# A decoder layer in fp32 on one core: SP's queue in another order, and half of k's moves on GpSimd

## The chip, the cores and the metric

The kernel runs on one core of one Trainium2 chip. The time is the device time of one execution in microseconds (us); several executions give a median. The core has five engines with instruction streams of their own: TensorE (PE, and PEld for its weight loads), VectorE (DVE), ScalarE (ACT), GpSimd (POOL) and SyncE (SP), which here only issues DMAs. They meet through semaphores.

## What is computed

One layer over x of 4 batches x 256 tokens x 256 channels, all in float32:

```
x = x + attention(layernorm(x))          # 32 heads of 64, 8 k/v heads, rotary embedding, causal
x = x + ssm(ctx, z = layernorm(x))       # selective scan over 256 steps, 256 channels, 16 states
x = x + ffn(layernorm(x))                # gate, up, down; int32 weights: (w - 128) * scale

attention: q, k, v = h Wq', h Wk', h Wv';  rope(q), rope(k);  softmax(q k' / 8, causal) v;  Wo
ssm:       u = silu(conv4(in_proj ctx));  dt, B, C = x_proj u;  delta = softplus(dt_proj dt + b)
           s_t = s_{t-1} exp(delta A) + delta u B_t;  y_t = s_t C_t;  (y + D u) silu(z)
ffn:       down(silu(gate h) * (up h))
```

## The kernel before, in words

Attention is cut into 32 **units** (UNITS, L36), one for each batch and k/v head; a unit holds the 4 q heads of its k/v head. Four units make a **k group** (KG): k is projected, rotated and moved for four units at once. The scan is cut into 32 pieces (16 states x 2 halves of the channels), laid under the units by the list SCANS (L56): none in units 0 to 3, then 1, 2, 1, 2, then one in each of units 8 to 28, and 2, 2, 1.

What TensorE does is written out in `unit` (L1171): transposes of the probabilities of unit u, the **scores** of unit u+1 (`scores`, L1031, its products at L1041), more transposes, pieces of the output projection (L1141), in the second unit of a group the projection (`fill`, L1028) of the next k group, in the third that of v, the product with v (L1123), and the projection of q for unit u+3. VectorE (`unit`, L850) rotates q for unit u+2 (`rope`, L698 and L699: two products, read from PSUM), scales the attention of unit u-1 (L809), takes the maxima of the scores of u+1 (L711), and runs the scan piece: the product with B (`drive`, L786), the scan (L793), in a group's second unit k's rotation (L701, L703), and the product with C (L799). ScalarE does the exponentials (L493), the copies out of PSUM (L499) and the scan's decays (L519). GpSimd (L443) adds the two halves of a rotation (`add_rope`, L418) and adds a scan piece to y (`add_y`, L424).

**Moves.** The rotation leaves q and k in `rc` with the two halves of a head in different places. Short DMAs of 32 KB bring them to `qt` and `kt`, where scores read them. For a unit's q these are 8 DMAs, 4 issued by SP and 4 by GpSimd (`move_heads`, L257, DMA at L266). For a k group these are 8 DMAs, all by SP (`move_k`, L295, DMA at L303); SP then waits for them and issues one more DMA of 256 KB that copies kt's lower 64 partitions to its upper ones (L306), the **doubling copy**, for which the group's first scores wait (`k_in`). The rotation buffer has two places, so VectorE's next rotation but one waits for the moves.

**SP's queue** (L273 to L364) is served in order, and a wait in it holds up all behind it. In the start: x, weights, k's moves and its copy, q's moves of units 0 and 1, more weights. Then B and C of the scan go out to DRAM and come back, broadcast to 128 partitions, as `bc` (two DMAs of 512 KB for each state, two buffers). Then q of unit 2, weights, q of unit 3, k group 1 with its copy, wo (2 MB), all the feed-forward weights and scales (L332 to L343), q of units 4 and 5, and the second bc. From unit 4 a loop (L349): q of unit u+2, in a group's second unit the next k group with wait and copy, and then the bc loads that unit u's own scans set free (L359, a wait for `hc_done`).

The integer weights are converted by VectorE at the end of unit 5 (gate, L821) and of unit 12 (up and down, L826, L830).

In the start ScalarE issues its loads, the last eight being Wq's for units 2 and 3 (L533), and then an activation that loads its table (L537, `act_warm`). GpSimd waits for that before it computes the layernorm's rstd (L393), and VectorE's normalisation (L681) waits for rstd.

## Time and profile before

| what | value |
|---|---|
| median of 3 runs | 524.07 us (522.26 to 529.78) |
| the profiled execution | 523.78 us, of which the profile's span is 522.0 us |
| busy: PE / PEld / DVE / ACT / POOL | 79% / 62% / 70% / 52% / 42% of the span |
| mean granted clock of TensorE | 0.912 |
| the chain that ended last, by engine | PE 33%, DVE 17%, issue 15%, SP's queue 12%, POOL 9%, DMA 7% |

Busy shares are means over the whole span. A unit starts with its scores: the time from one group of L1041 products to the next is the length of a unit. What ended an engine's idle time stands in brackets behind an instruction in the timeline, with the time it was idle. "SPq" marks a DMA's issue on SP's queue, which isn't counted as busy; a DMA lands later than it is issued.

### The profile page before, as it was taken

To read this page: it belongs to the slowest core of one execution; us is meant where nothing else is said; L and a number is where in the kernel's file an instruction comes from. 1 tells how busy PE (TensorE), PEld (TensorE's weight loads), DVE (VectorE), ACT (ScalarE), POOL (GpSimd) and SP (SyncE) were. 2 spreads that over 40 slices of the span, in tenths; PEclk is the share of its full clock that TensorE was granted. 3 is DMA by queue.
4 is the path that set the end of the run, shared out by engine and by line. 5 is a ranking of instruction groups with operands and counts; after the bars stand their busy time and mean duration, and the time that the engine had idled before them with its cause. 6 is when DMAs were issued, how large, how long until landed. Compare 5 with 4: busy or idle time off the path is not lost.

```text
span 522.0 us, 7681 instructions
## 1 busy us (share of the span) xinstructions
PE 414.5 (79%) x2604; PEld 325.4 (62%) x2636; DVE 366.6 (70%) x485; ACT 271.0 (52%) x779; POOL 221.3 (42%) x234
## 2 busy tenths in 40 slices
PE   3648987188768697987889799978998894659996
PEld 1433666166656476866777688757887773447774
DVE  2774357257999885897798679858767999755442
ACT  0514587046556465755666658645556665433321
POOL 1741232206464666446446635635464474310000
PEclk9787789687889799998999989989999997779999
DMA  9325324703151415201430521323042130000000
GB/s 223 74 56 96 113 51 131 230 10 98 37 170 55 156 31 153 96 11 46 133 102 24 144 91 48 76 87 102 21 133 74 57 102 0 2 0 21 20 22 20
DMA packets 51110, 40.63 MB, mean 78 GB/s; under 512 B 32280, under 2 KB 43744, under 8 KB 51072
## 3 DMA queue, kind: packets, MB, share of 16 engines
q1 hardware_dynamic: 40864, 34.48, 23.2%
q0 software_dynamic: 4096, 4.20, 3.4%
q10 hardware_dynamic: 6112, 1.47, 1.4%
q8 instruction: 21, 0.34, 0.3%
q14 instruction: 17, 0.14, 0.1%
HBM read 26.36 MB, written 1.18 MB: 53 GB/s over the span
## 4 chain that ended last, share of the span: by engine, by line
PE 33%; DVE 17%; issue 15%; SPq 12%; POOL 9%; DMA 7%; ACT 5%; ACTq 2%; DVEq 0%; POOLq 0%
PE ps_s L1041 6%; SPq L303 6%; PE ps_p L1028 6%; PE ps_p L1243 5%; DMA qt<-rc 4%; POOL rc L418 4%; DVE state L793 4%; PE ps_s L1228 3%; DVE nmax L711 3%; PE ps_p L1141 3%; PE ps_r L1095 3%; DVE state L786 3%; DMA kt<-rc 3%; SPq L266 2%; POOL y L424 2%
## 5 line engine op out<-in xcount | busy, mean ns | idle before, releaser
L493 ACT ACTIVATE prob<-ps_s,nmax 128x256 f32<-128x256 f32 (+1 forms) x256 | 104.8, 444 | 72.6 <-DVE nmax L711 72.6
L424 POOL TENSOR_TENSOR y<-y,state 128x1024 f32<-128x1024 f32 x32 | 80.3, 2510 | 112.2 <-DVE state L799 112.2
L418 POOL TENSOR_TENSOR rc<-rc,rs 128x512 f32<-128x512 f32 x40 | 57.7, 1442 | 104.0 <-DVE rs L699 70.4
L711 DVE TENSOR_REDUCE nmax<-ps_s 128x2 f32<-128x512 f32 (+1 forms) x96 | 60.3, 682 | 45.1 <-PE ps_s L1052 45.1
L499 ACT ACTIVATE pt<-ps_r 128x512 f32<-128x512 f32 x96 | 53.6, 593 | 58.1 <-PE ps_r L1095 54.5
L793 DVE TENSOR_TENSOR_SCAN state<-decay,state 128x1024 f32<-128x1024 f32 x32 | 81.5, 2546 | 2.3 <-ACT decay L519 1.2
L1041 PE MATMUL ps_s<-kt,qt 64*128 64x256 f32 (+1 forms) x512 | 55.5, 360 | 30.7 <-DMA qt<-rc 30.7
L1028 PE MATMUL ps_p<-xt_all,wq 128*128 128x256 f32 x256 | 71.2, 427 | 9.1 <-DVE rs L703 6.4
L1041 PEld LDWEIGHTS ps_s<-kt,qt 64*128 64x128 f32 x512 | 47.1, 201 | 38.2 <-DMA qt<-rc 32.5
L266 POOL DMA_DIRECT2D qt<-rc x128 | 63.8, 504 | 9.7 <-POOL rc L418 9.5
L1141 PE MATMUL ps_p<-wo,attn_t 128*128 128x256 f32 x256 | 61.7, 389 | 7.7 <-DVE x L816 4.1
L1095 PE MATMUL ps_r<-ident,prob 128*128 128x128 f32 x384 | 55.2, 282 | 14.8 <-ACT pt L499 12.6
L1028 PEld LDWEIGHTS ps_p<-xt_all,wq 128*128 128x128 f32 x256 | 51.5, 211 | 23.4 <-DVE rs L703 8.0
L1095 PEld LDWEIGHTS ps_r<-ident,prob 128*128 128x128 f32 x384 | 48.2, 147 | 20.3 <-ACT pt L499 13.2
L493 ACT ACTIVATION_READ_ACCUMULATOR prob<-ps_s,nmax 128x1 f32 x256 | 58.8, 230 | 0.0
L1141 PEld LDWEIGHTS ps_p<-wo,attn_t 128*128 128x128 f32 x256 | 47.8, 195 | 14.6 <-DVE x L816 4.8
L1123 PE MATMUL ps_o<-pt,vv 128*64 128x256 f32 x256 | 43.1, 415 | 12.5 <-ACT pt L499 12.4
L698 DVE TENSOR_TENSOR rc<-ps_p,cos_s 128x512 f32<-128x512 f32 x32 | 22.0, 689 | 34.0 <-PE ps_p L1028 23.0
L786 DVE TENSOR_TENSOR state<-du,bc 128x1024 f32<-128x1024 f32 x32 | 41.6, 1301 | 0.0
L799 DVE TENSOR_TENSOR state<-state,bc 128x1024 f32<-128x1024 f32 x32 | 38.8, 1214 | 0.2
L519 ACT ACTIVATE decay<-delta,a_neg 128x1020 f32<-128x1020 f32 x32 | 36.6, 1144 | 0.0
L506 ACT ACTIVATE x<-rinv 128x512 f32<-128x512 f32 x32 | 20.2, 631 | 22.7 <-DVE rinv L720 22.7
(110 smaller groups left out, 531.1 us busy)
## 6 DMA issues: line engine op xcount, KB each, us to landing
bc<-bc_scratch SPq DMA_DIRECT2D x32, 512.0 KB, 4.7
qt<-rc POOLq DMA_DIRECT2D x128, 32.0 KB, 1.7
qt<-rc SPq DMA_DIRECT2D x128, 32.0 KB, 2.0
kt<-rc SPq DMA_DIRECT2D x64, 32.0 KB, 1.8
kt<-kt SPq DMA_DIRECT2D x8, 256.0 KB, 3.0
wo<-wo_t SPq DMA_DIRECT2D x1, 2048.0 KB, 10.9
wq<-wqkv_t SPq DMA_DIRECT2D x24, 64.0 KB, 2.6
xs<-x SPq DMA_DIRECT2D x1, 1024.0 KB, 8.1
```

The source lines that it names most:

```text
L266: queue.dma_start(qt[to:to + HALF, u % 2, h // 2, :], rc[h * HALF:(h + 1) * HALF, r % 2, c, :]).then_inc(landed[u % 2], 16)
L418: nc.gpsimd.tensor_tensor(rc[:, r % 2, :, :], rc[:, r % 2, :, :], rs[:], ALU.add).then_inc(rope_add, 1)
L424: nc.gpsimd.tensor_tensor(y[:, v % 2, :], y[:, v % 2, :], state[:, v % 2, :], ALU.add).then_inc(state_free, 1)
L493: nc.scalar.activation(o, i, ACT.Exp, bias=nmax[:, r, c:c + 1], accum_out=rsum[:, r, GRP + head:GRP + head + 1]).then_inc(exp_done, 1)
L499: nc.scalar.activation(pt[:, fill, :], ps_r[:, fill % 2, :], ACT.Copy).then_inc(pt_copied, 1)
L711: nc.vector.tensor_reduce(nmax[:, u % 2, c:c + k], ps_s[:, part, :].rearrange("p (k s) -> p k s", k=k), AX.X, ALU.max, negate=True).then_i ...
L786: nc.vector.tensor_tensor(state[:, v % 2, :], du[:, v % 2, :], bc[:, n % 2, 0, :], ALU.mult).then_inc(drive_done, 1)
L793: nc.vector.tensor_tensor_scan(state[:, v % 2, :], decay[:, v % 2, :], state[:, v % 2, :], 0.0, ALU.mult, ALU.add).then_inc(decay_free, 1)
L1028: last = nc.tensor.matmul(o, lhs, rhs, start=(k == 0), stop=(k == KT - 1))
L1041: return nc.tensor.matmul(ps_s[:, bank, col:col + keys], qt[lo:lo + HD, r, h // 2, t * P:(t + 1) * P], kt[lo:lo + HD, j % 2, u % KG, 0:key ...
L1095: last = nc.tensor.transpose(ps_r[:, fill % 2, k * P:(k + 1) * P], src, ident[:])
L1141: last = nc.tensor.matmul(ps_p[:, 1, t * HID:(t + 1) * HID], attn_t[:, k, t * P:(t + 1) * P], wo[:, k, :], start=(k == 0 and t == 0), stop ...
```

## The change

SP's own list of work gets one form for all units. In unit u SP first issues its half of q's moves for unit u+2. In the third unit of a group (u % 4 == 2) the doubling copy of the next k group follows (`double_k`), then this unit's share of the loads (`load_wq`, wo in unit 2, `load_ffn` in units 4 to 8 and 11), then the bc loads for the scans of the unit before (u-1 instead of u), and in the second unit of a group SP's half of k's moves. Of k's 8 moves GpSimd issues 4, behind k's add. At the start SP issues q's moves for unit 0 between k's moves and k's copy. The conversion of the gate weights moves from unit 5 to unit 10, that of up and down from unit 12 to unit 14. ScalarE's first activation moves ahead of its last eight weight loads.

```diff
--- before.py
+++ after.py
@@ -186,8 +186,10 @@
         wq_in = [sem(f"wq_in{g}") for g in range(KVH)]
         wk_in = [sem(f"wk_in{j}") for j in range(2)]
         wv_in = sem("wv_in")
-        q_in = [sem(f"q_in{r}") for r in range(2)]
-        k_half = [sem(f"k_half{r}") for r in range(2)]
+        q_sp = [sem(f"q_sp{r}") for r in range(2)]
+        q_pool = [sem(f"q_pool{r}") for r in range(2)]
+        k_sp = [sem(f"k_sp{r}") for r in range(2)]
+        k_pool = [sem(f"k_pool{r}") for r in range(2)]
         k_in = [sem(f"k_in{r}") for r in range(2)]
         tab_ps, tab_sb = sem("tab_ps"), sem("tab_sb")
         up_in = sem("up_in")
@@ -249,12 +251,9 @@
                         queue.dma_start(wq[:, k, g, c, :].rearrange("p (h i) -> p h i", i=HALF), w_q[k, g, c]
                                         ).then_inc(wq_in[g], 16)
 
-        q_moves, k_moves = 2 * GRP, 2 * KG
-
-        half_moves = q_moves // 2
-        q_low = [sem(f"q_low{r}") for r in range(2)]
-
-        def move_heads(queue, u, heads, landed):
+        q_moves, k_moves = GRP, KG
+
+        def move_q(queue, u, heads, landed):
 
             r = ROPE_AT["q", u]
             queue.wait_ge(rope_add, r + 1)
@@ -266,6 +265,17 @@
                     queue.dma_start(qt[to:to + HALF, u % 2, h // 2, :], rc[h * HALF:(h + 1) * HALF, r % 2, c, :]
                                     ).then_inc(landed[u % 2], 16)
 
+        def move_k(queue, j, heads, landed):
+
+            r = ROPE_AT["k", j]
+            queue.wait_ge(rope_add, r + 1)
+            if j >= 2:
+                queue.wait_ge(score_done, 3 * KG * (j - 1))
+            for i in heads:
+                for c in range(2):
+                    queue.dma_start(kt[c * HALF:(c + 1) * HALF, j % 2, i, :],
+                                    rc[i * HALF:(i + 1) * HALF, r % 2, c, :]).then_inc(landed[j % 2], 16)
+
         block = ctx.enter_context(nc.Block())
 
 
@@ -288,26 +298,46 @@
                 sp.dma_start(xproj[:], xproj_t.rearrange("(e p) n -> p e n", p=P)).then_inc(ssm_in, 16)
                 sp.dma_start(dtproj[:], dtproj_t).then_inc(ssm_in, 16)
 
-            def move_q(u):
-
-                move_heads(sp, u, range(GRP // 2), q_low)
-
-            def move_k(j):
-
-                r = ROPE_AT["k", j]
-                sp.wait_ge(rope_add, r + 1)
-                if j >= 2:
-                    sp.wait_ge(score_done, 3 * KG * (j - 1))
-                for i in range(KG):
-                    for c in range(2):
-                        sp.dma_start(kt[c * HALF:(c + 1) * HALF, j % 2, i, :],
-                                     rc[i * HALF:(i + 1) * HALF, r % 2, c, :]).then_inc(k_half[j % 2], 16)
-                sp.wait_ge(k_half[j % 2], 16 * k_moves * (j // 2 + 1))
+            def double_k(j):
+
+                sp.wait_ge(k_sp[j % 2], 16 * k_moves * (j // 2 + 1))
+                sp.wait_ge(k_pool[j % 2], 16 * k_moves * (j // 2 + 1))
                 sp.dma_start(kt[HD:P, j % 2, :, :], kt[0:HD, j % 2, :, :]).then_inc(k_in[j % 2], 16)
 
-            move_k(0)
-            move_q(0)
-            move_q(1)
+            def load_bc(n):
+
+                for c in range(2):
+                    sp.dma_start(bc[:, n % 2, c, :], bc_scratch[c * NS + n:c * NS + n + 1, :].to_broadcast([P, L])
+                                 ).then_inc(bc_in[n % 2], 16)
+
+            full = P * (HT - 1)
+
+            def load_ffn(u):
+
+                if u == 4:
+                    sp.dma_start(wgu_i[:], wgate_t.rearrange("(k p) n -> p k n", p=P)).then_inc(ffn_in, 16)
+                elif u == 5:
+                    sp.dma_start(wdn_i[:, 0:HT - 1, :], wdown_t[0:full, :].rearrange("(k p) n -> p k n", p=P)
+                                 ).then_inc(ffn_in, 16)
+                    sp.dma_start(sdn[:], s_down.rearrange("(a n) -> a n", a=1).to_broadcast([P, HID])
+                                 ).then_inc(ffn_in, 16)
+                elif u == 6:
+                    sp.dma_start(wdn_i[0:HP[-1], HT - 1, :], wdown_t[full:HF, :]).then_inc(ffn_in, 16)
+                elif u in (7, 8):
+                    i, v = (0, s_gate) if u == 7 else (1, s_up)
...
+                elif u == 11:
+                    sp.wait_ge(wq_done, 1)
+                    sp.dma_start(wgu_i[:], wup_t.rearrange("(k p) n -> p k n", p=P)).then_inc(up_in, 16)
+
+            move_k(sp, 0, range(KG // 2), k_sp)
+            move_q(sp, 0, range(GRP // 2), q_sp)
+            double_k(0)
+            move_q(sp, 1, range(GRP // 2), q_sp)
             with nc.allow_non_contiguous_dma(reason="weights by the halves of a head, once"):
                 load_wk(1)
             load_wq(sp, 4)
@@ -316,52 +346,26 @@
             sp.wait_ge(xdbl_sb, 2)
             sp.dma_start(bc_scratch, xdbl[DR:XR, :]).then_inc(bc_out, 16)
             sp.wait_ge(bc_out, 16)
...
             load_bc(0)
-            move_q(2)
-            load_wq(sp, 6)
-            load_wq(sp, 7)
-            move_q(3)
-            move_k(1)
-            sp.dma_start(wo[:], wo_t.rearrange("(k p) n -> p k n", p=P)).then_inc(wo_in, 16)
-            sp.dma_start(wgu_i[:], wgate_t.rearrange("(k p) n -> p k n", p=P)).then_inc(ffn_in, 16)
-            full = P * (HT - 1)
-            sp.dma_start(wdn_i[:, 0:HT - 1, :], wdown_t[0:full, :].rearrange("(k p) n -> p k n", p=P)
-                         ).then_inc(ffn_in, 16)
...
-            sp.dma_start(sdn[:], s_down.rearrange("(a n) -> a n", a=1).to_broadcast([P, HID])
-                         ).then_inc(ffn_in, 16)
-            move_q(4)
-            move_q(5)
-            sp.wait_ge(ssm_ready, 5)
-            load_bc(1)
-            for u in range(4, UNITS):
+            for u in range(UNITS):
                 if u + 2 < UNITS:
-                    move_q(u + 2)
-                if u % KG == 1 and u // KG + 1 < GROUPS:
-                    move_k(u // KG + 1)
-                for v in scans(u):
+                    move_q(sp, u + 2, range(GRP // 2), q_sp)
+                if u % KG == 2 and u // KG + 1 < GROUPS:
+                    double_k(u // KG + 1)
+                if u < 2:
+                    load_wq(sp, 6 + u)
+                if u == 2:
+                    sp.dma_start(wo[:], wo_t.rearrange("(k p) n -> p k n", p=P)).then_inc(wo_in, 16)
+                load_ffn(u)
+                for v in scans(u - 1) if u else ():
                     if v % 2 == 1 and v // 2 + 2 < NS:
                         sp.wait_ge(hc_done, v + 1)
-                        n = v // 2
-                        for c in range(2):
-                            sp.dma_start(bc[:, n % 2, c, :],
-                                         bc_scratch[c * NS + n + 2:c * NS + n + 3, :].to_broadcast([P, L])
-                                         ).then_inc(bc_in[n % 2], 16)
-                if u == 7:
-                    sp.wait_ge(wq_done, 1)
-                    sp.dma_start(wgu_i[:], wup_t.rearrange("(k p) n -> p k n", p=P)).then_inc(up_in, 16)
+                        load_bc(v // 2 + 2)
+                if u % KG == 1 and u // KG + 1 < GROUPS:
+                    move_k(sp, u // KG + 1, range(KG // 2), k_sp)
+                if u == 3:
+                    sp.wait_ge(ssm_ready, 5)
+                    load_bc(1)
 
             for b in range(B):
                 sp.wait_ge(res_done, b + 1)
@@ -425,10 +429,11 @@
                                         ).then_inc(state_free, 1)
 
             add_rope(("k", 0))
+            move_k(nc.gpsimd, 0, range(KG // 2, KG), k_pool)
             add_rope(("q", 0))
-            move_heads(nc.gpsimd, 0, range(GRP // 2, GRP), q_in)
+            move_q(nc.gpsimd, 0, range(GRP // 2, GRP), q_pool)
             add_rope(("q", 1))
-            move_heads(nc.gpsimd, 1, range(GRP // 2, GRP), q_in)
+            move_q(nc.gpsimd, 1, range(GRP // 2, GRP), q_pool)
 
             def x1_rstd(lo, hi, step):
 
@@ -446,9 +451,10 @@
                         add_y(v)
                 if u + 2 < UNITS:
                     add_rope(("q", u + 2))
-                    move_heads(nc.gpsimd, u + 2, range(GRP // 2, GRP), q_in)
+                    move_q(nc.gpsimd, u + 2, range(GRP // 2, GRP), q_pool)
                 if u % KG == 1 and u // KG + 1 < GROUPS:
                     add_rope(("k", u // KG + 1))
+                    move_k(nc.gpsimd, u // KG + 1, range(KG // 2, KG), k_pool)
                 if u == UNITS - 3:
                     x1_rstd(0, LAST, 2)
             for v in scans(UNITS - 1):
@@ -530,11 +536,11 @@
                     nc.scalar.dma_start(sin_raw[:, t, :].rearrange("p (h i) -> p h i", i=HALF), pick[t, 1]
                                         ).then_inc(tab_in, 16)
             nc.scalar.dma_start(par[:], ssm_par.rearrange("(e p) n -> p e n", p=P)).then_inc(par_in, 16)
+
+            act.wait_ge(consts, 2)
+            nc.scalar.activation(rstd2[:], eps[:], ACT.Silu).then_inc(act_warm, 1)
             load_wq(nc.scalar, 2)
             load_wq(nc.scalar, 3)
-
-            act.wait_ge(consts, 2)
-            nc.scalar.activation(rstd2[:], eps[:], ACT.Silu).then_inc(act_warm, 1)
 
             act.wait_ge(consts, 6)
             for i in range(2 * EB):
@@ -688,10 +694,11 @@
                 if r >= 2:
                     kind, i = ROPES[r - 2]
                     if kind == "q":
-                        dve.wait_ge(q_low[i % 2], 16 * half_moves * (i // 2 + 1))
-                        dve.wait_ge(q_in[i % 2], 16 * half_moves * (i // 2 + 1))
+                        dve.wait_ge(q_sp[i % 2], 16 * q_moves * (i // 2 + 1))
+                        dve.wait_ge(q_pool[i % 2], 16 * q_moves * (i // 2 + 1))
                     else:
-                        dve.wait_ge(k_half[i % 2], 16 * k_moves * (i // 2 + 1))
+                        dve.wait_ge(k_sp[i % 2], 16 * k_moves * (i // 2 + 1))
+                        dve.wait_ge(k_pool[i % 2], 16 * k_moves * (i // 2 + 1))
                 if r >= 1:
                     dve.wait_ge(rope_add, r)
                 if f[0] == "q":
@@ -875,9 +882,9 @@
                     times_c(v)
                 if u < 4:
                     prepare_scan(u)
-                if u == 5:
+                if u == 10:
                     dequantise_gate()
-                if u == 12:
+                if u == 14:
                     dequantise_up_down()
                 if u == UNITS - KVH // 2:
                     x1_stats(0, LAST)
@@ -1031,8 +1038,8 @@
             def scores(u):
 
                 r, j = u % 2, u // KG
-                pe.wait_ge(q_low[r], 16 * half_moves * (u // 2 + 1))
-                pe.wait_ge(q_in[r], 16 * half_moves * (u // 2 + 1))
+                pe.wait_ge(q_sp[r], 16 * q_moves * (u // 2 + 1))
+                pe.wait_ge(q_pool[r], 16 * q_moves * (u // 2 + 1))
                 pe.wait_ge(k_in[j % 2], 16 * (j // 2 + 1))
 
                 def dot(bank, col, h, t, keys, start=False):
```

## Rows read from the trace of the kernel before

**Rows 1.** Waits of TensorE, 28 to 450 us: engine, line, us in total, times, longest.

```profile
PE ps_s L1041 <- DMA qt<-rc: 30.7, 7, 11.4
```

**Rows 2.** Timeline of TensorE, score products: start, us, instruction, [idle before <-releaser].

```profile
40.32 2.93 PE L1041 MATMUL ps_s<-kt,qt 64*128 64x256 f32 x16 [7.38 <-DMA qt<-rc]
...
102.89 2.93 PE L1041 MATMUL ps_s<-kt,qt 64*128 64x256 f32 x16 [11.35 <-DMA qt<-rc]
...
206.55 1.74 PE L1041 MATMUL ps_s<-kt,qt 64*128 64x256 f32 x16 [2.90 <-DMA qt<-rc]
...
255.27 1.58 PE L1041 MATMUL ps_s<-kt,qt 64*128 64x256 f32 x16 [1.43 <-DMA qt<-rc]
```

**Rows 3.** Windows: length, then PE, PEld, DVE, ACT, POOL busy, PEclk, DMA, GB/s.

```profile
206.50:217.10 10.60, 10.33 (x68) 8.51 (x69) 7.35 (x9) 5.40 (x20) 3.00 (x4) 0.84 0.17 48
217.10:226.00 8.90, 8.85 (x69) 7.27 (x69) 8.15 (x10) 7.06 (x23) 4.25 (x7) 1.00 0.38 122
226.00:243.10 17.10, 12.49 (x75) 9.96 (x75) 14.61 (x21) 7.00 (x23) 10.08 (x8) 0.90 0.08 19
...
243.10:255.30 12.20, 10.71 (x77) 8.82 (x77) 9.61 (x12) 9.06 (x26) 6.82 (x8) 1.00 0.49 147
255.30:264.20 8.90, 8.85 (x68) 7.27 (x69) 7.06 (x8) 5.55 (x21) 2.74 (x6) 1.00 0.13 32
...
274.70:285.90 11.20, 10.64 (x75) 8.79 (x75) 9.19 (x12) 7.05 (x23) 6.91 (x8) 1.00 0.10 25
```

**Rows 4.** Timeline of SP's queue, around units 2 and 10.

```profile
78.60 4.95 SPq L303 DMA_DIRECT2D kt<-rc  x8
...
99.12 4.98 SPq L266 DMA_DIRECT2D qt<-rc  x8
...
192.46 4.94 SPq L303 DMA_DIRECT2D kt<-rc  x8
198.69 0.50 SPq L306 DMA_DIRECT2D kt<-kt  x1
...
200.60 7.29 SPq L266 DMA_DIRECT2D qt<-rc  x8
```

**Rows 5.** Timeline of GpSimd, in the start and around units 2 and 10.

```profile
28.24 1.27 POOL L418 TENSOR_TENSOR rc<-rc,rs 128x512 f32<-128x512 f32 x1 [3.47 <-DVE rs L703]
...
82.67 1.27 POOL L418 TENSOR_TENSOR rc<-rc,rs 128x512 f32<-128x512 f32 x1 [4.10 <-DVE rs L699]
...
190.19 2.24 POOL L418 TENSOR_TENSOR rc<-rc,rs 128x512 f32<-128x512 f32 x1 [4.28 <-DVE rs L703]
192.39 2.37 POOL L424 TENSOR_TENSOR y<-y,state 128x1024 f32<-128x1024 f32 x1
194.72 1.28 POOL L418 TENSOR_TENSOR rc<-rc,rs 128x512 f32<-128x512 f32 x1
196.29 1.99 POOL L266 DMA_DIRECT2D qt<-rc  x4 [0.29 <-POOL rc L418]
```

**Rows 6.** Timeline of VectorE, three instructions.

```profile
136.60 2.29 DVE L786 TENSOR_TENSOR state<-du,bc 128x1024 f32<-128x1024 f32 x1
...
196.59 1.21 DVE L786 TENSOR_TENSOR state<-du,bc 128x1024 f32<-128x1024 f32 x1
...
226.24 4.25 DVE L830 SCALAR_TENSOR_TENSOR wdn_i<-wdn_i,sdn 128x256 f32<-128x256 int32 x6
```

**Rows 7.** The page's DMA issues: count, KB each, median us from issue to landing.

```profile
kt<-kt SPq DMA_DIRECT2D x8, 256.0 KB, 3.0
wo<-wo_t SPq DMA_DIRECT2D x1, 2048.0 KB, 10.9
```

**Rows 8.** Timeline of the start: ScalarE's queue, VectorE, GpSimd.

```profile
5.58 7.28 ACTq L249 DMA_DIRECT2D wq<-wqkv_t  x8
...
11.54 0.64 DVE L677 BATCH_NORM_AGGREGATE mv<-stats 128x2 f32<-128x6 f32 x8
...
14.47 0.20 POOL L393 TENSOR_SCALAR rstd<-mv 128x8 f32<-128x8 f32 x1 [11.42 <-ACT rstd L537]
```

More of the change, by code:

```diff
@@ new lines, in _ @@
+            full = P * (HT - 1)
[11 more added lines that the diff above has]
+                    i, v = (0, s_gate) if u == 7 else (1, s_up)
+                    with nc.allow_non_contiguous_dma(reason="704 scales, once"):
+                        sp.dma_start(sgu[:, i, 0:HT - 1], v[0:full].rearrange("(k p) -> p k", p=P)
+                                     ).then_inc(ffn_in, 16)
+                        sp.dma_start(sgu[0:HP[-1], i, HT - 1:HT], v[full:HF].rearrange("(p k) -> p k", k=1)
+                                     ).then_inc(ffn_in, 16)
+                elif u == 11:
+                    sp.wait_ge(wq_done, 1)
+                    sp.dma_start(wgu_i[:], wup_t.rearrange("(k p) n -> p k n", p=P)).then_inc(up_in, 16)
@@ L355, in _ @@
                     if v % 2 == 1 and v // 2 + 2 < NS:
                         sp.wait_ge(hc_done, v + 1)
-                        n = v // 2
-                        for c in range(2):
-                            sp.dma_start(bc[:, n % 2, c, :],
-                                         bc_scratch[c * NS + n + 2:c * NS + n + 3, :].to_broadcast([P, L])
-                                         ).then_inc(bc_in[n % 2], 16)
-                if u == 7:
-                    sp.wait_ge(wq_done, 1)
-                    sp.dma_start(wgu_i[:], wup_t.rearrange("(k p) n -> p k n", p=P)).then_inc(up_in, 16)
+                        load_bc(v // 2 + 2)
```

10 lines of the change are left out of this document (removed).

## The prediction, made before the kernel was changed

> **What bounds the kernel now.** I read the waits of every engine first, then the timeline of TensorE's score products, then SP's and GpSimd's timelines around the gaps found, last the windows between two scores. Inside a unit no engine is the bound alone: in the unit from 217.1 to 226.0 us TensorE is busy 8.85 of 8.90 us and VectorE 8.15, at full clock [rows 3]. So 8.9 us is the floor of a unit, and what stands above it is gaps. TensorE waits seven times, 30.7 us in all, for q's moves [rows 1]: 7.38 us before the scores of unit 0, 11.35 before those of unit 4, and five shorter ones before units 12, 16, 20, 24 and 28, every time the first unit of a new k group (unit 12: 2.90, unit 16: 1.43; units 20 and 24 are as 12, unit 28 as 16, together 12.0) [rows 1, 2].
>
> The reason is one queue. At 192.46 SP issues eight moves of k (4.94 us, 0.62 each), waits for them, issues the doubling copy at 198.69 and two loads of B and C, and only at 200.60 the moves of q for unit 12 [rows 4]; the add that makes that q ended at 196.00, and GpSimd issues its own half from 196.29 [rows 5]. At unit 4 it is worse: q's add ends at 83.94 [rows 5], but SP, with k's moves from 78.60 and then all the feed-forward loads, gets to q at 99.12 [rows 4].
>
> **The change, part by part.** I work on the profiled execution (523.78 us, span 522.0, beside a median of 524.07), times in us on its axis.
>
> *Gap at unit 4.* In the new order q's moves for unit 4 leave at 84.0 and need four issues, 2.5; the doubling copy goes at 86.5, takes 0.5 to issue and 3.0 to land [rows 7]: 90.0. The copy is issued last and is the larger, so it lands last. TensorE was ready at 102.89 - 11.35 = 91.54 [rows 2]. The gap goes whole, and nothing late takes its place with a margin of 1.5. VectorE has the scan's preparation behind this gap and moves forward with it. Gain 11.4. What can take some back is wo, 2 MB, issued right behind the copy at about 87.5 and landing 10.9 later [rows 7], so at 98.4: q's moves for unit 5 are issued meanwhile, at about 95.5, behind it in SP's rings, and are due near 101. I set 0 to 2 for that, with the term for B and C below.
>
> *Gaps at units 12, 16, 20, 24, 28.* Here GpSimd counts. Before, it adds k (190.19 to 192.43), adds to y (to 194.76), and adds q (to 196.00) [rows 5]. Now four k moves stand behind k's add, at the price of its q moves, 1.99 and 0.3 ahead of them [rows 5]: 2.3. y's add then ends at 197.1 and q's at 198.4. From there SP needs 2.5 + 0.5 + 3.0 = 6.0: 204.4. There is a second cost. GpSimd's adds and VectorE's operations with two operands in SBUF take turns: k's add took 2.24 against 1.27 undisturbed [rows 5], VectorE's product L786 2.29 beside such an add against 1.21 alone [rows 6]. The shifted y add now ends in the middle of L786 (196.59 on), which waits for it and then goes ahead of q's add: that ends near 199.5, the copy lands at 205.5. TensorE is ready at 203.65 and started at 206.55 [rows 2]. So of 2.9 only 1.1 to 2.2 is gained, and 0.8 to 1.9 stays as a wait for k's copy.
>
> The clock adds to it: the unit behind the 2.90 gap took 10.60 at a granted clock of 0.84, the one behind the gap of 1.43 took 8.90 at 1.00, that is at the upper of the two levels (2.4 GHz) throughout [rows 3]. A remaining gap of 0.8 to 1.9 lies nearer the second: I take 1.2 of the 1.7. Three gaps of the first kind give 3 x (1.65 + 1.2) = 8.5, bounds 3.3 (1.1 each and no clock) and 13.8 (2.9 + 1.7 each). At 16 and 28 the same shift ends 0.8 before to 0.3 behind TensorE's readiness: 2.5 for both, bounds 2 and 3. VectorE's delayed product and scan cost 1.7 in the unit, most of it in idle time: minus 2 over seven groups. Sum 9.0, bounds 3 and 16.
>
> *GpSimd's queue as a risk.* Its four moves from 196.29 ran in 1.99 although VectorE's L786 (196.59) ran beside them [rows 5, 6]. That is the price I use. The Trainium skill speaks against a part of the change here: its page "SBUF — State Buffer", under "Who interferes with whom" and in the box on the "DVE blocks DMA" trap, says that a DMA issued by GpSimd has its descriptors written by that engine, which VectorE can lock out of the shared port pair in its two-port modes, and advises the hardware queues instead; its figures are about 620 ns alone and 3100 ns overlapped. By that, four moves would cost some 10 us more per group and the time would rise by tens of us. The rows disagree as far as they go; the page itself says that a product of two operands is no two-port mode.
>
> *Start.* ScalarE issues eight weight loads from 5.58 to 12.86 before the activation on which GpSimd waits: its rstd begins at 14.47, after waiting 11.42 for it; the statistics were done at 12.18 [rows 8]. With the activation first, rstd starts at 12.2: 2.3 gained, and more where the norms no longer meet GpSimd's convolution, at most the 3.47 that GpSimd idled before k's first add [rows 5], since that convolution then bounds it. I take 2.8. From that add to unit 0's scores the chain was 8 moves, landing, copy, 4 moves, landing: 29.5 to 40.32, 10.8 [rows 2, 5]. Now GpSimd does four k moves (2.3) and q's add (1.5), then SP four q moves 2.5, copy 0.5, landing 3.0: 9.8. Gain 1.0, bounds 0 and 1.5. Together 3.8, bounds 2 and 5.
>
> *Conversions.* Unit 13 lasted 17.10 where the same kind of unit takes 11.20, with VectorE in the conversion block (4.25 for the down matrix, behind the up matrix) [rows 3, 6]: 5.9 lost. The block moves to the end of unit 14, whose stretch (243.1 to 255.3) had 2.6 of VectorE's time free [rows 3]. So about 3.3 stay to be paid; gain 2.5 with the gate's short conversion included, bounds 0 and 4.
>
> *B and C, loads spread.* A pair of loads now leaves a unit later, behind q's moves. In the steady part the buffer isn't read for three units, so 9 us or more remain. At units 6 and 7, with two scans, the second load lands about when it is read: minus 1.0 together with wo, bounds 0 and minus 3. The spread loads themselves are needed units later and cost nothing.
>
> **Sum.** 3.8 + 11.4 + 9.0 + 2.5 - 1.0 = 25.7; 523.8 - 25.7 = 498.1. I forecast 498.
>
> **Rivals.** (a) The k copy, now last behind q, takes over the wait at the later groups, and the clock still falls: that part gives nothing. For it: two adds and a 3.0 us landing stand in its chain; against it: 1.1 even with the turn-taking. 523.8 - 3.8 - 11.4 - 2.5 + 1.0 = 507. (b) The adds don't meet and all gaps go: the later groups give 16 and start and conversions their upper ends, 5 and 4, and nothing is paid: 523.8 - 16 - 11.4 - 5 - 4 = 487, or 488 with the 1.0 for B and C. (c) The conversions cost more in their new place and wo holds unit 5's q up to its full landing: minus 3 there and nothing of the 2.5, with (a) beside it: 512 to 515. (d) Slower than before: GpSimd's k moves are held up by VectorE. If each of the four waits out one product of 1.21 [rows 6] they end 4.8 later: the copy lands at about 210, 3.4 behind the old start of unit 12. Over six groups that is minus 20, the clock falls at two more (minus 3.4), and unit 4 loses 2 of its margin: 3.8 + 9.4 + 2.5 - 1.0 - 20.4 - 3.4 = minus 9: 533. It decides from about 3.5 us more per group than my 2.3. Against it: the 1.99 beside L786. That the change doesn't do what it says I find nowhere: the waits count the halves, and the spread loads are all issued before their readers.
>
> **Chances.** Forecast 0.57, (a) 0.20, (b) 0.15, (c) 0.05, (d) 0.03. Time 498; range 488 to 510, which leaves out the end of (b), (c) and (d). A measurement can tell this kernel from the old one at about 2%, that is from 513.6 down and 534.5 up. Faster by over 2%: 0.94; within: 0.05; slower: 0.01.
>
> **What would show it.** Right: scores of unit 4 start near 87 (91.5 less the start's gain), with no wait; the waits of TensorE for qt or kt fall from 30.7 to under 13, most of that at unit 0; SP issues q's moves within 0.1 of the add in all units; GpSimd's k moves take 2.0; units behind 12, 20 and 24 take 8.9. Wrong: a wait for kt of 2 or more in every group with the clock at 0.84 behind it (a), k moves on GpSimd over 3 us (d), VectorE waiting for bc, or unit 15 above 15 us.

## The result and the profile after

The changed kernel takes **488.0 us** (median of 4 runs, 486.4 to 489.4) against 523.8 for the kernel before, a ratio of 0.930 with a 95% interval from 0.922 to 0.937. The forecast was 498, with 488 as the low end of the range: the direction was right and the gain of 36 us is 10 larger than the 25.7 I had added up. The profiled execution has a span of 486.8 beside 522.0.

TensorE's waits, 28 to 450 us, in the kernel after (engine, line, us in total, times, longest), where [rows 1] had 30.7 us in seven:

```profile
PE ps_s L1048 <- DMA kt<-kt: 8.0, 5, 6.0
```

One of these five is the wait before unit 0 (6.0); the other four share 2.0 us. The timeline of the score products, where it answers to [rows 2]:

```profile
34.88 2.93 PE L1048 MATMUL ps_s<-kt,qt 64*128 64x256 f32 x16 [5.99 <-DMA kt<-kt]
...
85.44 1.58 PE L1048 MATMUL ps_s<-kt,qt 64*128 64x256 f32 x16
...
183.97 1.58 PE L1048 MATMUL ps_s<-kt,qt 64*128 64x256 f32 x16 [0.50 <-DMA kt<-kt]
...
224.10 1.58 PE L1048 MATMUL ps_s<-kt,qt 64*128 64x256 f32 x16 [0.42 <-DMA kt<-kt]
```

The gap of 11.35 at unit 4 is gone, that of 2.90 at unit 12 is 0.50, and the transfer waited for is now k's copy, issued last, instead of q's moves. Units 20 and 24 wait 0.65 and 0.47, unit 28 not at all. These are signs that the prediction named for being right: scores of unit 4 near 87 and no wait before them, waits under 13 in all, most of it at unit 0, and stretches of 8.9 behind units 12, 20 and 24.

The windows between two scores (us, busy PE, PEld, DVE, ACT, POOL, then the granted clock, DMA share, GB/s), to be laid beside [rows 3]:

```profile
62.30:73.40 11.10, 9.09 (x69) 7.22 (x69) 6.82 (x12) 10.74 (x27) 5.78 (x8) 1.00 0.27 52
85.40:96.60 11.20, 8.87 (x60) 7.08 (x60) 7.95 (x13) 5.73 (x21) 3.25 (x5) 0.85 0.45 138
...
184.00:192.90 8.90, 8.85 (x68) 7.25 (x69) 8.48 (x11) 6.49 (x22) 5.46 (x7) 1.00 0.57 176
...
224.10:237.80 13.70, 10.40 (x68) 8.27 (x69) 12.97 (x18) 6.61 (x22) 6.60 (x7) 0.88 0.28 79
```

Behind unit 12's scores the clock is 1.00 throughout and the stretch is at the floor of 8.90, where it took 10.60 at 0.84. The fourth window is the price of the conversions in their new place: VectorE is busy 12.97 of 13.70.

From the starts of the scores in both traces the 35.2 us of span divide as follows (a stretch runs from one unit's scores to the next one's; times of before, then after):

| stretch | before | after | gained |
|---|---|---|---|
| start to scores of 2 | 66.88 | 62.33 | 4.6 (5.4 at unit 0) |
| 2 to 3 | 12.67 | 11.03 | 1.6 (clock) |
| 3 to 4 (the large gap) | 23.34 | 12.08 | 11.3 |
| 4 to 8 (clock and gate's conversion before) | 52.50 | 49.80 | 2.7 |
| 8 to 11 | 37.56 | 37.53 | 0.0 |
| 11 to 12, 15 to 16, 19 to 20, 23 to 24, 27 to 28 (the gaps) | 67.18 | 57.19 | 10.0 |
| 12 to 13, 20 to 21, 24 to 25 (clock behind them) | 31.60 | 26.71 | 4.9 |
| 14 to 15 (conversions before) | 17.16 | 11.21 | 6.0 |
| 16 to 17 (conversions after) | 8.91 | 13.66 | -4.8 |
| scores of 31 to the end | 97.06 | 98.11 | -1.1 |

The stretches not named agree within 0.1. How one group now runs is seen around unit 10. SP's queue:

```profile
172.27 2.41 SPq L276 DMA_DIRECT2D kt<-rc  x4
178.16 2.41 SPq L265 DMA_DIRECT2D qt<-rc  x4
180.67 0.54 SPq L305 DMA_DIRECT2D kt<-kt  x1
181.25 1.27 SPq L310 DMA_DIRECT2D bc<-bc_scratch  x2
```

GpSimd:

```profile
170.00 2.24 POOL L422 TENSOR_TENSOR rc<-rc,rs 128x512 f32<-128x512 f32 x1 [4.28 <-DVE rs L710]
172.54 1.99 POOL L276 DMA_DIRECT2D kt<-rc  x4 [0.30 <-POOL rc L422]
174.54 2.37 POOL L428 TENSOR_TENSOR y<-y,state 128x1024 f32<-128x1024 f32 x1
176.85 1.29 POOL L422 TENSOR_TENSOR rc<-rc,rs 128x512 f32<-128x512 f32 x1
178.43 1.99 POOL L265 DMA_DIRECT2D qt<-rc  x4 [0.29 <-POOL rc L422]
```

VectorE:

```profile
176.41 2.82 DVE L793 TENSOR_TENSOR state<-du,bc 128x1024 f32<-128x1024 f32 x1
179.26 2.29 DVE L800 TENSOR_TENSOR_SCAN state<-decay,state 128x1024 f32<-128x1024 f32 x1
```

The reader is to see three things. SP issues q's moves 0.02 us behind the end of q's add (176.85 + 1.29 = 178.14), where it came 4.60 late before [rows 4, 5]. GpSimd's k moves cost the 1.99 that its q moves cost (in the first two groups 2.23 and 2.52). And the two adds run back to back (the second starts at 176.85) while VectorE's product, issued in the middle of the first at 176.41, takes 2.82 where it takes 1.21 alone [rows 6]. That fits a product that stands back until both adds are through; the adds take no longer than before (2.37 and 1.28 [rows 5]).

### The profile page after: what moved, and what is told of

It reads as the page before. It is cut to its first block, busy times and chain, and to the rows that moved or that the text cites. A ratio compares the mean times of both kernels' runs of the same rounds, so it can differ in the third digit from the quotient of the medians.

```text
span 486.8 us, 7703 instructions
## 1 busy us (share of the span) xinstructions
PE 405.3 (83%) x2604; PEld 318.1 (65%) x2636; DVE 373.2 (77%) x485; ACT 271.2 (56%) x779; POOL 237.5 (49%) x266
## 4 chain that ended last, share of the span: by engine, by line
PE 41%; DVE 19%; issue 13%; POOL 11%; ACT 7%; DMA 5%; SPq 3%; DVEq 0%; ACTq 0%; POOLq 0%
PE ps_p L1035 7%; PE ps_s L1048 6%; PE ps_p L1148 5%; PE ps_p L1250 5%; PE ps_s L1235 4%; POOL rc L422 4%; DVE state L800 4%; PE ps_r L1102 4%; DVE nmax L718 4%; DVE state L793 3%; POOL y L428 3%; PE ps_o L1130 3%; ACT prob L499 3%; DMA kt<-kt 2%; SPq L265 2%
## 5 line engine op out<-in xcount | busy, mean ns | idle before, releaser
L800 DVE TENSOR_TENSOR_SCAN state<-decay,state 128x1024 f32<-128x1024 f32 x32 | 79.4, 2483 | 2.3 <-ACT decay L525 1.2
L1035 PE MATMUL ps_p<-xt_all,wq 128*128 128x256 f32 x256 | 70.2, 421 | 9.2 <-DVE rs L710 6.4
L1148 PE MATMUL ps_p<-wo,attn_t 128*128 128x256 f32 x256 | 63.4, 397 | 7.2 <-DVE x L823 4.1
L1035 PEld LDWEIGHTS ps_p<-xt_all,wq 128*128 128x128 f32 x256 | 50.5, 208 | 23.3 <-DVE rs L710 8.3
L1102 PE MATMUL ps_r<-ident,prob 128*128 128x128 f32 x384 | 54.0, 278 | 12.8 <-ACT pt L505 11.2
L1048 PE MATMUL ps_s<-kt,qt 64*128 64x256 f32 (+1 forms) x512 | 52.2, 344 | 8.0 <-DMA kt<-kt 8.0
L1102 PEld LDWEIGHTS ps_r<-ident,prob 128*128 128x128 f32 x384 | 46.6, 144 | 18.0 <-ACT pt L505 12.1
L1048 PEld LDWEIGHTS ps_s<-kt,qt 64*128 64x128 f32 x512 | 44.7, 192 | 15.0 <-issue 13.9
L793 DVE TENSOR_TENSOR state<-du,bc 128x1024 f32<-128x1024 f32 x32 | 49.7, 1553 | 0.2 <-DMA bc<-bc_scratch 0.2
L806 DVE TENSOR_TENSOR state<-state,bc 128x1024 f32<-128x1024 f32 x32 | 40.8, 1276 | 0.2
```

What stands on the lines that cost most here:

```text
L793: nc.vector.tensor_tensor(state[:, v % 2, :], du[:, v % 2, :], bc[:, n % 2, 0, :], ALU.mult).then_inc(drive_done, 1)
L800: nc.vector.tensor_tensor_scan(state[:, v % 2, :], decay[:, v % 2, :], state[:, v % 2, :], 0.0, ALU.mult, ALU.add).then_inc(decay_free, 1)
L1035: last = nc.tensor.matmul(o, lhs, rhs, start=(k == 0), stop=(k == KT - 1))
L1048: return nc.tensor.matmul(ps_s[:, bank, col:col + keys], qt[lo:lo + HD, r, h // 2, t * P:(t + 1) * P], kt[lo:lo + HD, j % 2, u % KG, 0:key ...
L1102: last = nc.tensor.transpose(ps_r[:, fill % 2, k * P:(k + 1) * P], src, ident[:])
L1148: last = nc.tensor.matmul(ps_p[:, 1, t * HID:(t + 1) * HID], attn_t[:, k, t * P:(t + 1) * P], wo[:, k, :], start=(k == 0 and t == 0), stop ...
```

## The experiments

All spans are of profiled executions, ratios are against the kernel before. The repeat, the old order, all of k on SP and the copy first ran on one chip, with the kernel before at 524.8 us; the loads at once, the activation, the conversions in pieces and B and C alone on a second (523.7); the split alone, the spread alone and the best on a third (524.8). Between chips the ratios and the single stretches are compared, not the last microsecond.

### The same code again: how much of a stretch is noise

> The changed kernel again, as the measure for the others of this call. Expected 488, ratio 0.93, span near 487, scores of unit 12 at 184.0 with a wait of 0.5 for the copy of kt.

Measured: 487.1 us, 0.929 [0.923, 0.934], span 484.7. Two of its windows, behind the scores of units 2 and 16:

```profile
61.10:73.80 12.70, 10.91 (x68) 8.43 (x67) 7.14 (x12) 11.14 (x27) 5.70 (x8) 0.87 0.23 43
223.60:235.80 12.20, 8.94 (x67) 7.38 (x67) 12.17 (x17) 6.56 (x22) 5.17 (x6) 1.00 0.28 86
```

The stretch from unit 2 to 3 is 1.6 longer than in the first run of the same code (12.70 at a clock of 0.87 against 11.03 at 1.00), the one from 16 to 17 is 1.4 shorter (12.23 at 1.00 against 13.66 at 0.88). So the 1.6 "gained" at unit 2 belongs to the execution, not to the change, and single stretches of the first 10 units tell nothing below 1.7 us. The sum of the four stretches from 4 to 8 is 49.8 in both. The wait before unit 12 is 1.01 here, where it was 0.50: single waits for the copy move by half a microsecond too.

### What holds the later gaps: the order of SP's queue, or the split of k's moves

**The old order in the new kernel.** In SP's loop:

```diff
-                if u + 2 < UNITS:
-                    move_q(sp, u + 2, range(GRP // 2), q_sp)
                 if u % KG == 2 and u // KG + 1 < GROUPS:
                     double_k(u // KG + 1)
+                for v in scans(u - 1) if u else ():
...
+                        load_bc(v // 2 + 2)
+                if u + 2 < UNITS:
+                    move_q(sp, u + 2, range(GRP // 2), q_sp)
                 if u < 2:
                     load_wq(sp, 6 + u)
...
                 load_ffn(u)
-                for v in scans(u - 1) if u else ():
...
-                        load_bc(v // 2 + 2)
```

> The changed kernel with SP's doubling copy and its B and C loads ahead of q's moves again, as they stood before; all else as changed. Theory O (the order in SP's queue closed the later gaps): q's moves of unit 12 leave only after the two loads, share the DMA engines with them and land about 1.2 us after TensorE is ready; with that and the lower clock behind it some 3 to 8 us come back, 490 to 496. Theory K (splitting k's moves closed them): no change within 1 us.

Measured: 491.7 us, 0.937 [0.931, 0.943], span 489.7. The waits for q are back, 8.3 us in sum against 12.0 in the kernel before; units 12, 20 and 24 wait half as long as there or less, units 16 and 28 longer (2.83 for 1.43, 1.85 for 1.51):

```profile
184.19 1.58 PE L1048 MATMUL ps_s<-kt,qt 64*128 64x256 f32 x16 [1.34 <-DMA qt<-rc]
226.73 2.93 PE L1048 MATMUL ps_s<-kt,qt 64*128 64x256 f32 x16 [2.83 <-DMA qt<-rc]
359.42 2.60 PE L1048 MATMUL ps_s<-kt,qt 64*128 64x256 f32 x16 [1.85 <-DMA qt<-rc]
```

Units 20 and 24 wait 1.41 and 0.83. Against the repeat 5.0 us of span are lost. From unit 11's scores to unit 31's this kernel takes 220.7 us, the changed one 215.9, the one before 232.0: of 16.1 gained in that part, the gaps and the conversions together, 11.3 stay without the order. (The repeat takes 214.9 for that part.)

**All of k's moves on SP in the new kernel**, in the loop as shown and likewise at the start for group 0 (what the waits count follows):

```diff
-                    move_k(nc.gpsimd, u // KG + 1, range(KG // 2, KG), k_pool)
...
-                    move_k(sp, u // KG + 1, range(KG // 2), k_sp)
+                    move_k(sp, u // KG + 1, range(KG), k_sp)
```

> The changed kernel with all eight moves of k on SP's queue again, GpSimd moving q alone; order as changed. Theory O: SP issues k for 5 us where it is idle, q's add on GpSimd comes 2.3 us earlier and q's moves wait about 1.4 us for SP, so the copy lands within 0.5 us of where it does now: 486 to 490. Theory K: each later group waits 2.5 us more and the clock falls behind it: 500 to 510.

Measured: 484.5 us, 0.923 [0.918, 0.927], span 482.6: faster than the change. Unit 0's scores start at 35.81, 1.4 later than in the repeat (34.40), but the waits at 12, 20, 24 and 28 are gone and 16 waits 0.25. It also lies below the 486 to 490 that I expected. Of 3.9 us gained on the repeat from unit 11 to unit 31, 2.4 are waits and 1.4 the stretch behind unit 16, which differs by as much between two executions of the same code. In the new order the split is a loss of some 2 us: it helps only at the start.

**The copy ahead of q's moves.** 

```diff
-                if u + 2 < UNITS:
-                    move_q(sp, u + 2, range(GRP // 2), q_sp)
                 if u % KG == 2 and u // KG + 1 < GROUPS:
                     double_k(u // KG + 1)
+                if u + 2 < UNITS:
+                    move_q(sp, u + 2, range(GRP // 2), q_sp)
```

> The changed kernel with the doubling copy ahead of q's moves and the B and C loads still behind them. If the wait that is left (kt's copy, 0.4 to 0.65 us at units 12 to 24) is only its place in the queue, it goes: minus 2 us, 486. Rival: the copy's transfer delays q's moves by as much and nothing changes.

Measured: 486.0 us, 0.925 [0.921, 0.930], span 484.7. All waits from unit 4 on are gone, and the stretches that end at units 12, 16, 20 and 24 take 10.63, as at 12, 20 and 24 with k on SP. The window behind unit 16 takes it back:

```profile
221.90:237.40 15.50, 11.77 (x68) 9.18 (x67) 13.40 (x19) 7.04 (x23) 8.04 (x7) 0.78 0.19 58
```

There the conversions meet a clock of 0.78. Why it fell in this run I can't say: no gap precedes it.

**Each part alone on the kernel before.** The loads of B and C behind q's moves:

```diff
                 if u + 2 < UNITS:
                     move_q(u + 2)
-                if u % KG == 1 and u // KG + 1 < GROUPS:
-                    move_k(u // KG + 1)
-                for v in scans(u):
+                for v in scans(u - 1):
...
+                if u % KG == 1 and u // KG + 1 < GROUPS:
+                    move_k(u // KG + 1)
```

> The kernel before with one thing changed: the B and C loads a unit later, behind q's moves (k's eight moves on SP, its wait and copy ahead of q, all loads in a block). Theory O': the two loads between the copy and q's moves are most of the later gaps, 1.3 us of issue and 2 us of shared transfer: waits at units 12 to 28 fall from 2.9 and 1.4 to under 0.6 and 0, the clock stays at its upper level behind them, and the gaps' share, some 13 of 36 us, is gained alone: 511. Theory K': SP's five us of k moves and its wait for them are what matters: 520 or more.

Measured: 506.3 us, 0.970 [0.961, 0.980], span 504.8. SP's queue at unit 12's q, in place of [rows 4], and the score products:

```profile
190.60 4.97 SPq L303 DMA_DIRECT2D kt<-rc  x8
196.98 0.50 SPq L306 DMA_DIRECT2D kt<-kt  x1
197.57 2.47 SPq L266 DMA_DIRECT2D qt<-rc  x4
200.09 1.40 SPq L357 DMA_DIRECT2D bc<-bc_scratch  x2
```

```profile
101.31 2.93 PE L1041 MATMUL ps_s<-kt,qt 64*128 64x256 f32 x16 [11.40 <-DMA qt<-rc]
...
202.11 1.58 PE L1041 MATMUL ps_s<-kt,qt 64*128 64x256 f32 x16 [0.31 <-DMA qt<-rc]
...
247.81 1.58 PE L1041 MATMUL ps_s<-kt,qt 64*128 64x256 f32 x16
```

Before, the two loads stood between the copy and q, a line of that queue beside [rows 4]:

```profile
199.24 1.27 SPq L359 DMA_DIRECT2D bc<-bc_scratch  x2
```

k's eight moves and the copy still stand ahead of q; only the two B and C loads left, and the later gaps are closed but for 0.31. Unit 11 runs 1.86 earlier here; on a common axis q's moves leave 1.2 earlier than before (200.60 - 1.86 - 197.57), while the gap shrinks by 2.6. The other 1.4 is the landing: SP's four moves of unit 12 land a median of 3.8 us after their issue in the kernel before and 2.4 here, where no load of 512 KB is issued ahead of them. k's moves and the copy go on holding q, for 3.4 of the 4.6 us by which it was late; but TensorE isn't ready before 203.65 on the old axis, and that lateness fits in ahead of it. What turned it into a gap were the two loads, and not the whole list, as [rows 4] let me believe.

From unit 11 to unit 31 it takes 215.3 us, 16.7 less than before and as little as the whole change (215.9), although the conversions are in their old place.

Half of k's moves on GpSimd, order as before; GpSimd issues the rest behind k's add:

```diff
-                for i in range(KG):
+                for i in range(KG // 2):
...
             add_rope(("k", 0))
+            pool_k(0)
...
                     add_rope(("k", u // KG + 1))
+                    pool_k(u // KG + 1)
```

> The kernel before with one part: half of k's moves by GpSimd, order of SP's queue as before. SP is through with k 2.5 us earlier, but q's add comes 2.3 us later; the copy and the two loads still stand ahead of q. Theory S (SP's time is what counts): the gap at unit 4 shrinks by 2.5, at unit 12 from 2.9 to 1.2, at 16 and 28 it does not shrink, the clock stays up behind 12, 20 and 24: 510 to 514. Rival (GpSimd's queue counts): q is as late as before, 520 to 524.

Measured: 507.3 us, 0.965 [0.961, 0.968], span 506.4. Its score products of units 0, 4, 12, 16 and 28:

```profile
37.66 2.93 PE L1056 MATMUL ps_s<-kt,qt 64*128 64x256 f32 x16 [5.30 <-DMA qt<-rc]
95.07 2.93 PE L1056 MATMUL ps_s<-kt,qt 64*128 64x256 f32 x16 [8.29 <-DMA qt<-rc]
194.74 1.58 PE L1056 MATMUL ps_s<-kt,qt 64*128 64x256 f32 x16 [1.10 <-DMA qt<-rc]
241.00 2.43 PE L1056 MATMUL ps_s<-kt,qt 64*128 64x256 f32 x16 [2.16 <-DMA qt<-rc]
374.52 2.81 PE L1056 MATMUL ps_s<-kt,qt 64*128 64x256 f32 x16 [2.27 <-DMA qt<-rc]
```

Unit 16 waits longer than before (2.16 for 1.43), unit 28 too (2.27 for 1.51), where I had expected them unchanged, and the time is below the 510 to 514 expected. Up to unit 11 it has gained 10.0 (2.7 of it at unit 0, 3.1 of the wait at unit 4, 1.6 each at unit 2, which the repeat shows to be chance, and behind unit 4), from there to unit 31 7.0. So at the later gaps the two loads moved alone bring 16.7, the split alone 7.0, and the changed kernel with both 16.1 together with its conversions: two remedies for one gap, and the order needs no help.

### The gap at unit 4

**Loads spread and wo behind q, alone on the kernel before** (`load_ffn` as in the change and the gate's conversion in unit 10):

```diff
-            sp.dma_start(wo[:], wo_t.rearrange("(k p) n -> p k n", p=P)).then_inc(wo_in, 16)
-            sp.dma_start(wgu_i[:], wgate_t.rearrange("(k p) n -> p k n", p=P)).then_inc(ffn_in, 16)
...
             move_q(4)
+            sp.dma_start(wo[:], wo_t.rearrange("(k p) n -> p k n", p=P)).then_inc(wo_in, 16)
             move_q(5)
...
                     move_q(u + 2)
+                load_ffn(u)
```

> The kernel before with one part: wo behind q's moves of unit 4 and the feed-forward loads spread over units 4 to 8 and 11 (the gate's conversion therefore in unit 10); k all on SP, its copy and the B and C loads ahead of q as before. If the 11.4 us at unit 4 are the loads' place in the queue and nothing else, they go whole: scores of unit 4 at 91.5, time 512. The later gaps stay at 2.9 and 1.4. Rival: k's eight moves and copy ahead of q are part of it and 2 to 4 us of the gap stay: 515.

Measured: 511.9 us, 0.973 [0.970, 0.977], span 510.5. Its score products of units 4 and 12:

```profile
91.40 1.58 PE L1050 MATMUL ps_s<-kt,qt 64*128 64x256 f32 x16
...
191.26 2.93 PE L1050 MATMUL ps_s<-kt,qt 64*128 64x256 f32 x16 [3.01 <-DMA qt<-rc]
```

No wait at unit 4, which starts at 91.40, within 0.14 of the 91.54 at which I had TensorE ready; unit 8 starts at 141.29 where it was 155.40. That is 14.1: 11.5 for the gap and 2.6 more behind it. The later gaps stay and are no shorter (3.01, 2.75, 2.39, 3.46 and 1.64 at units 12 to 28; I had expected 1.4 at unit 16), and from unit 11 to unit 31 this kernel takes 2.5 longer than the one before.

**The loads all at once behind q for unit 4, in the new kernel:**

```diff
-    load_ffn(u)
+    for w in ((4, 5, 6, 7, 8) if u == 2 else (11,) if u == 11 else ()):
+        load_ffn(w)
```

> The changed kernel with all the feed-forward loads issued in unit 2, right behind wo, as before. If the 11.4 us at unit 4 came from q's moves of unit 4 standing behind the loads, they do not come back, since these moves and the copy go first here: scores of unit 4 near 85.8. But q's moves of unit 5 now wait for some 13 us of issuing: they leave near 95 instead of 89 and the scores of unit 5 start 3 us late: 489 to 492. Rival: the transfers themselves hold up what follows, the scores of unit 5 come 8 us or more late: 495 or more.

Measured: 486.2 us, 0.932 [0.922, 0.942], span 484.4, no loss against the repeat (0.929 [0.923, 0.934]). The damage is seen at the score products of unit 5, and healed:

```profile
85.79 1.58 PE L1049 MATMUL ps_s<-kt,qt 64*128 64x256 f32 x16
97.88 1.58 PE L1049 MATMUL ps_s<-kt,qt 64*128 64x256 f32 x16 [2.49 <-DMA qt<-rc]
```

Unit 5 waits 2.49 for q, which SP issues at 93.32 behind the loads; the two stretches from unit 5 to 7 then take 8.79 and 11.21, where the repeat has 12.89 and 12.89. Spreading the loads over the units is worth nothing measurable; that they stand behind q for unit 4 is the whole gain. I had expected a loss of some us here and was wrong.

### Start and conversions

**ScalarE's activation in its old place**, behind the last eight weight loads:

```diff
-            act.wait_ge(consts, 2)
-            nc.scalar.activation(rstd2[:], eps[:], ACT.Silu).then_inc(act_warm, 1)
             load_wq(nc.scalar, 2)
             load_wq(nc.scalar, 3)
+            act.wait_ge(consts, 2)
+            nc.scalar.activation(rstd2[:], eps[:], ACT.Silu).then_inc(act_warm, 1)
```

> The changed kernel with ScalarE's first activation behind its last eight weight loads again. rstd starts 2.3 us later. The start's first add of k moves from 24.1 to 26.5 or later, scores of unit 0 from 34.6 to 37 to 38: plus 2.3 to 3.5 us, 490.

Measured: 491.2 us, 0.943 [0.935, 0.951], span 488.3. GpSimd's timeline in its start, to be laid beside [rows 8] and [rows 5]:

```profile
14.01 0.20 POOL L397 TENSOR_SCALAR rstd<-mv 128x8 f32<-128x8 f32 x1 [10.95 <-ACT rstd L544]
...
27.34 1.26 POOL L422 TENSOR_TENSOR rc<-rc,rs 128x512 f32<-128x512 f32 x1 [3.05 <-DVE rs L711]
```

In the changed kernel these two start at 12.07 and 24.10, in the repeat at 11.80 and 23.61. Unit 0's scores start at 38.11 instead of 34.88 and 34.40: the place of one small activation is 3.2 to 3.7 us.

**The conversion block in seven pieces** at the end of units 14, 15, 16, 18, 19, 20 and 22 (`dequantise_piece(i)` is one of its seven instructions):

```diff
-    if u == 14:
-        dequantise_up_down()
+    if u in (14, 15, 16, 18, 19, 20, 22):
+        dequantise_piece((14, 15, 16, 18, 19, 20, 22).index(u))
```

> The changed kernel with the conversion of the up and down matrices cut into its seven instructions, one at the end of each of units 14, 15, 16, 18, 19, 20 and 22. The block of 5.0 us costs unit 16 to 17 between 3.3 and 4.8 us over the 8.9 it takes else. Theory: VectorE has 0.4 to 0.8 us free in a unit, so single instructions of 0.71 hide almost whole: minus 3 us, 484. Rival: VectorE is the bound of these units and the same 5 us are paid in pieces: 488 to 489.

Measured: 482.8 us, 0.926 [0.918, 0.934], span 481.9. The ratio alone doesn't tell it from the repeat (0.929 [0.923, 0.934]); the stretches do. That behind unit 16 is at 8.90, where the block takes 12.2 and 13.7 in the two executions of the change, and those that got the pieces are as they were: the block has room if it comes in pieces.

### The best of it

The split kept for group 0 alone, k's moves all on SP from group 1 on (what the waits count follows), conversions in pieces:

```diff
-                    move_k(nc.gpsimd, u // KG + 1, range(KG // 2, KG), k_pool)
...
-                    move_k(sp, u // KG + 1, range(KG // 2), k_sp)
+                    move_k(sp, u // KG + 1, range(KG), k_sp)
...
-                if u == 14:
-                    dequantise_up_down()
+                if u in (14, 15, 16, 18, 19, 20, 22):
+                    dequantise_piece((14, 15, 16, 18, 19, 20, 22).index(u))
```

> The changed kernel with three edits from these runs: k's moves halved with GpSimd only for group 0, all on SP later, and the conversions of up and down one instruction at a time. Theory: the parts add. Scores of unit 0 near 34.6 as now (the run with all of k on SP: 35.8), no wait for kt's copy from unit 12 on (minus 2 us), the conversions hidden (minus 3.3): span 479 to 480, time 481. Rival: without the block of conversions nothing of the copy's margin is left and the waits return: 484.

Measured: **480.7 us**, 0.915 [0.912, 0.918], span 480.1, below both kernels. In the timeline of its score products one wait is left behind unit 0:

```profile
34.67 2.93 PE L1054 MATMUL ps_s<-kt,qt 64*128 64x256 f32 x16 [6.08 <-DMA kt<-kt]
...
224.22 1.58 PE L1054 MATMUL ps_s<-kt,qt 64*128 64x256 f32 x16 [0.59 <-DMA kt<-kt]
```

## Why the prediction was right in kind and short by 10 us

**Gap at unit 4 (11.4): right.** 11.3 came (stretch 3 to 4), and the spread alone reproduces it (11.5). The sentence that nothing late takes its place held, with wo behind the copy.

**Gaps at 12 to 28 (9.0): the step that failed.** The table gives 10.0 + 4.9 = 14.9, near the upper bound of 16 that I had given to rival (b). Three sizes inside it were wrong. First, I had VectorE's product go ahead of q's add, so that the add ended at 199.5 on the old axis, 7.1 behind the end of k's add. It ended at 178.14, 5.9 behind k's (172.24): the two adds ran back to back, and the product waited. The copy, issued at 180.67, let the scores start at 183.97, and 0.4 to 0.7 stayed as gap (1.0 at unit 12 in the repeat) instead of 0.8 to 1.9. So units 12, 20 and 24 gained 2.40, 2.28 and 2.72 instead of 1.65 each, which is 2.5 of the 5.9 that were missing; units 16 and 28 gave the 2.5 forecast. The kernel with only the split shows the same order: its product took 2.81 beside both adds. Second, with gaps that short the clock came back whole: 1.6 at three units (4.9) instead of 1.2 each (3.6), another 1.3. Third, the 2.0 I charged for VectorE's delay doesn't appear: the product lost 1.6, and the stretch from 11 to 12 still took 11.20 with 0.50 of it the gap, the stretch behind it 8.90. This is rival (b)'s end state by another way: it said that the adds don't meet, and the adds still keep VectorE waiting, only in the order that costs nothing.

**B, C and wo (-1.0): wrong sign.** Units 4 to 8 gained 2.7. I had priced the gap of 11.35 by its length and left out the clock behind it: before, unit 4 to 5 took 10.05 at a granted clock of 0.70 and 5 to 6 took 14.19 at 0.76; with the spread alone they took 9.52 at 1.00 and 12.90 at 0.87, and the repeat is within 0.1 of that (the first run of the change divides the same 49.8 otherwise). That is 1.8. The other 0.9 is the conversion of the gate weights, which the change and the spread alone both took out of the stretch from 7 to 8. It is this line of the kernel before, and that stretch took 15.38 with it, also when only B and C had moved, and 14.58 and 14.50 without it (spread alone, repeat):

```profile
144.44 0.89 DVE L821 TENSOR_SCALAR wgu<-wgu_i 128x1408 f16<-128x1408 int32 x1
```

So the term is +1.8, and the 0.9 belongs to the conversions. The cost that I feared was real but small: in the first trace of the change VectorE's product waits 0.17 for B and C at 139.13.

**Start (3.8): 5.4 at unit 0, 4.6 two units later.** The activation was under-sized: rstd came 2.4 earlier, as worked out, but k's add 4.1 earlier, not 2.8 (3.2 to 3.7 us when undone alone). The split of the first moves gave 1.3 to 1.4 for my 1.0.

**Conversions (2.5): 2.1, or 3.5 in the repeat.** Up and down gave 6.0 in the stretch from 14 to 15 (the prediction calls it unit 13) and cost 4.8 or 3.3 in the one from 16 to 17; the gate gave the 0.9. The part for the down matrix, 4.25 us, begins at 223.74 and so falls behind the scores of unit 16 (224.10), not before them; I had read the free time of the stretch ahead.

By terms: 14.9 for 9.0 (+5.9), 1.8 for -1.0 (+2.8), the start at unit 2 4.6 for 3.8 (+0.8), unit 2's clock +1.6, which is chance, since the repeat doesn't have it, conversions -0.4, the tail -1.1, and the gap 0.1 less. Together 9.5, the difference between 25.7 and the 35.2 of span.

**The rivals.** (a), the copy takes over the wait and the clock still falls, named the right transfer and the wrong size: the copy is what TensorE waits for, by 0.5. (b) gave 487 to 488, which is the time measured, and named the later gaps' worth well, 16 for 14.9; but its mechanism, adds that don't meet, is not what the trace shows, and its sum met in part by luck: it had nothing for the 1.8 behind unit 4 and the 1.6 of unit 2's clock, and too much for the start (5 for 4.6) and the conversions (4 for 2.1). (d), GpSimd's k moves held up, fell: they took 1.99 in the later groups. The Trainium skill's caution that I weighed (page "SBUF — State Buffer", under "Who interferes with whom") is about VectorE's two-port modes; here GpSimd's q moves at 178.43 took the same 1.99 with the end of a 1024-wide product and a scan beside them, which are not the operations it names. Two of GpSimd's issues of k moves were longer, both beside a TENSOR_SCALAR of VectorE: 2.23 at 25.67, and 2.52 at 72.14, where VectorE ran two over 128x1024. The trace doesn't show in which mode these ran, and no run tests it; the most that it cost was 0.5 us for four moves.

**What neither theory had.** [rows 4] show SP issue k's moves, copy, B and C and then q, and I blamed the whole list. Two loads were enough: with them behind q, k's moves and the copy could stay. Alone, the four parts sum to more than the whole in span: 17.2 + 11.5 + 15.6 on the kernel before and 3.7 (at unit 0) for the activation, 48 beside 35.2. Most of the excess lies where two parts close one gap: 16.7 + 7.0 for the 14.9 of the later gaps, and at unit 4 the 11.5 of the loads and 3.1 of the split for 11.3.

What stays open: why the clock fell behind unit 16 with the copy first (0.78) and why the same code gets 0.87 or 1.00 at unit 2. The first ends the comparison of copy first and q first without a verdict. That VectorE's product stood back for both adds is read from durations in two kernels; no run was made to separate it from other causes.

## What to carry to other kernels

When a queue delivers late, look for an entry right ahead of the late one that is needed later than what it blocks, and move that alone first (the two loads here waited for nothing, SP issued them 0.05 us behind the copy; they took issue time and lengthened q's landing); here two loads behind q gave 16.7 of 35 us, and a second remedy for the same gap did not add. Count a gap that goes with the clock behind it, not by its length alone. And before charging two engines for slowing each other, ask which of them is on the path: here the one that lost 1.6 us had them to spare.
